# A two-layer graph network on one core: the permutation and the plan of layer two moved into the placing steps, one-hots built from a 16-bit table in SBUF, and two transposes put in front of the relation product

## The reference, cut to what matters

```python
# layer one
msg = h[edge_src] + relvectors[edge_rel]
red = jax.ops.segment_sum(msg, edge_dst, num_segments=h.shape[0])
x = _layernorm(x + _gru_cell(red, h, w_ih, w_hh, b_ih, b_hh))
# layer two
deg_rsqrt = jax.lax.rsqrt(deg)
vals = deg_rsqrt[src] * deg_rsqrt[dst]
msgs = vals[:, None] * (x @ W.T)[dst]
out = jax.ops.segment_sum(msgs, src, num_segments=N)
x = _layernorm(x + out)
```

## Time and profile before

| | |
|---|---|
| time, median of 3 runs (lowest to highest) | 2451.86 us (2450.61 to 2453.98) |
| the profiled execution's own time | 2450.72 us |
| its span, first to last instruction | 2448.7 us |
| busy in the span | PE 2001.0, PE weight loads 1548.1, DVE 1745.1, ACT 831.4, POOL 1628.2 us |
| first and last gather of layer one | 56.1 and 1238.0 us |
| first and last gather of layer two | 1366.2 and 2410.7 us |

### The profile page before, as it was taken

One profiled execution on the slowest core, in us unless ns is written; L12 is line 12 of the kernel. 1 busy time (PEld: TensorE's weight loads), 2 busy tenths in 40 slices (PEclk: granted clock), 3 DMA queues, 4 the chain that ended last, 5 costly groups with the idle time before them and its releaser, 6 DMA issues.

```text
span 2448.7 us, 43994 instructions
## 1 busy us (share of the span) xinstructions
PE 2001.0 (82%) x10013; PEld 1548.1 (63%) x10013; DVE 1745.1 (71%) x2996; ACT 831.4 (34%) x3093; POOL 1628.2 (66%) x1767
## 2 busy tenths in 40 slices
PE   2489898879989769999997589888888888877773
PEld 2366666657666547777774477767676777665552
DVE  5678787788868668888875577767784787544674
ACT  4000000023323226767654366516560665200002
POOL 3677777777777745655510577777777777777774
PEclk7699999989989879999999699999999999999997
DMA  3244444444444335444442433333333333333334
GB/s 97 84 123 149 140 148 143 146 127 149 144 139 145 112 104 148 145 137 141 141 124 79 141 106 107 105 105 106 106 105 105 106 106 105 105 106 106 104 105 149
DMA packets 131522, 296.52 MB, mean 121 GB/s; under 512 B 31024, under 2 KB 64914, under 8 KB 131304
## 3 DMA queue, kind: packets, MB, share of 16 engines
q0 software_dynamic: 80016, 219.06, 31.0%
q10 hardware_dynamic: 35100, 57.62, 7.2%
q1 hardware_dynamic: 16188, 17.21, 2.2%
HBM read 260.91 MB, written 32.85 MB: 120 GB/s over the span
## 4 chain that ended last, share of the span: by engine, by line
PE 34%; POOL 26%; issue 14%; ACT 8%; DMA 8%; DVE 6%; DVEq 1%; SPq 1%; POOLq 0%; ACTq 0%
POOL rows L540 25%; PE ps L1542 19%; ACT rows L1333 6%; DMA rows<-gdram,ids 6%; PE ps L1639 4%; PE ps L1680 3%; DVE rows L700 3%; PE ps L1699 2%; PE ps L1682 2%; PE ps L1671 1%; SPq L398 1%; ACT sums L1482 1%; PE ps L1606 1%; DVEq L761 1%; PE ps L1669 1%
## 5 line engine op out<-in xcount | busy, mean ns | idle before, releaser
L1542 PE MATMUL ps<-rows,onehot 128*128 x5632 | 1372.2, 400 | 206.2 <-SPq L389 124.2
L1542 PEld LDWEIGHTS ps<-rows,onehot 128*128 128x128 f32 x5632 | 1085.8, 197 | 434.3 <-issue 256.2
L540 POOL DMA_INDIRECT rows<-in_x_dram,ids x832 | 796.5, 957 | 344.8 <-issue 245.0
L540 POOL DMA_INDIRECT rows<-gdram,ids x832 | 788.8, 948 | 246.7 <-issue 212.4
L796 DVE TENSOR_TENSOR sums<-sums,ps 128x256 f32 x400 | 168.2, 420 | 332.4 <-PE ps L1542 323.0
L1333 ACT ACTIVATE rows<-rows,a 128x128 f16<-128x128 f16 x624 | 190.8, 388 | 365.7 <-DVE rows L700 365.7
L766 DVE SCALAR_TENSOR_TENSOR onehot<-tkey,node_p,ps 128x512 f32<-128x512 f32 x403 | 298.4, 741 | 13.4 <-issue 10.2
L813 DVE TENSOR_TENSOR sums<-ps,sums 128x800 f16<-128x800 f32 (+1 forms) x156 | 216.3, 1414 | 1.3 <-issue 1.3
L706 DVE SCALAR_TENSOR_TENSOR onehot<-tkey,node_p,ps 128x1024 f32<-128x1024 f32 x154 | 195.7, 1271 | 1.4 <-issue 1.3
L1333 ACT ACTIVATE rows<-rows,b 128x128 f16<-128x128 f16 x624 | 189.5, 386 | 0.0
L1280 ACT COPY sums<-ps 128x256 f32<-128x256 f32 x49 | 18.2, 372 | 502.9 <-PE ps L1598 491.6
(11 more groups left out here) (271 smaller groups left out, 1875.3 us busy)
## 6 DMA issues: line engine op xcount, KB each, us to landing
xpd<-sums ACTq DMA_DIRECT2D x48, 384.0 KB
sums<-xpd ACTq DMA_DIRECT2D x48, 384.0 KB, 3.9
rows<-in_x_dram,ids POOLq DMA_INDIRECT x832, 2.8
rows<-gdram,ids POOLq DMA_INDIRECT x832
xt<-in_x_dram ACTq DMA_DIRECT2D x96, 128.0 KB, 2.2
gdram<-sums ACTq DMA_DIRECT2D x48, 128.0 KB, 1.8
out_dram<-sums SPq DMA_DIRECT2D x6, 896.0 KB
sums<-gdram SPq DMA_DIRECT2D x4, 896.0 KB
```

Of the source, the lines that this page charges most:

```text
L540: pool.indirect_dma_start(rows[:, at:at + D], None, source, bass.IndirectOffsetOnAxis(ap=ids[:, p, s * h + k:s * h + k + 1], axis=0)).then ...
L1542: prod = M.matmul(ps[:, h, 0:width], onehot[:, u % U, k, :], rows[:, bass.ds(at + k * stride, width)], start=(k == 0), stop=(k == q - 1))
```

## The change

Three things are changed. First, the counting is squeezed into 45 steps (52 rounds, so seven steps hold two), the closing of the counts takes two steps, and placing starts at step 55; the plan of layer two and the split of the places are cut into pieces beside placing steps 56 to 62 and later; the first 24 of the 26 batches of chunk 0 lie beside steps 63 to 111, one in two steps, and only two stay in the node steps. Second, the one-hots of counting, placing and permutation are built from `iota_k`, a 16-bit table in SBUF, and from 16-bit keys, and they lie with the key's number innermost; PE, ACT and a reduction on DVE read them and the products with a stride (8 or 16 elements). The 1024- and 512-wide one-hots of the steps themselves (L706, L766) are as before. Third, `sums_over` does its two transposes first and then its two relation products. Besides, POOL's loop for layer two is written chunk by chunk, with the index copy of a chunk's first turn behind the last gathers of the chunk before.

```diff
+COUNTING = 45
+CLOSE = FIRST + COUNTING
+PLACE = CLOSE + 2
+PLAN = PLACE + 1
+PERMUTE = PLACE + 8
+BATCHES = (WIN - PERMUTE) // 2
+SPLIT_LAG = 5
...
+        iota_k = sb("iota_k", [P, G, PB], F16)
...
-        oh_lo = early(2, SUB, P, dt=F16)
-        oh_hi = early(2, SUB, B, dt=F16)
+        oh_lo = early(2, P, SUB, dt=F16)
+        oh_hi = early(2, B, SUB, dt=F16)
...
+            turns = NG1 // S1
+            for g in range(CH):
+                a = g * turns
+                stage(1, S1 * H1, s_tix, a, a % 2)
+                with pool.Fori(0, turns // 2) as i:
+                    for p in range(2):
+                        issue(1, gdram[:, :], S1, H1, D, s_tix, i * 2 + (a + p), (a + p) % 2)
+                issue(1, gdram[:, :], S1, H1, D, s_tix, a + turns - 1, a % 2, False)
...
+                step(V.tensor_copy(hi_16, mask))
+                step(V.scalar_tensor_tensor(a32[:, :], mask, -float(P), lo1, ALU.mult, ALU.add))
+                step(V.tensor_copy(lo_16, a32[:, :]))
+                note(V.tensor_copy(iota_k[:, :, :], iota[:, 0:G].rearrange("p (a k) -> p a k", k=1).to_broadcast([P, G, PB])))
...
             def one_hot(out_ap, keys, count, width):
-                    out_ap, ps[:, 6, 0:width].rearrange("p (a v) -> p a v", a=1).to_broadcast([P, count, width]),
-                    keys.rearrange("p (k a) -> p k a", a=1).to_broadcast([P, count, width]), ALU.is_equal)
+                    out_ap, iota_k[:, 0:width, 0:count],
+                    keys.rearrange("p (v k) -> p v k", v=1).to_broadcast([P, width, count]), ALU.is_equal)
...
             def round_hots(out_ap, keys, r, width):
-                now = keys.rearrange("p (g w) -> p g w", g=CH)[:, :, bass.ds(r * each, each)]
+                now = keys.rearrange("p (g w) -> p g w", g=CH)[:, :, r * each:(r + 1) * each]
                 return V.tensor_tensor(
-                    out_ap.rearrange("p (g i) v -> p g i v", g=CH),
-                    ps[:, 6, 0:width].rearrange("p (g i v) -> p g i v", g=1, i=1).to_broadcast([P, CH, each, width]),
-                    now.rearrange("p g (i v) -> p g i v", v=1).to_broadcast([P, CH, each, width]), ALU.is_equal)
+                    out_ap.rearrange("p v (g i) -> p v g i", g=CH),
+                    iota_k[:, 0:width, 0:each].rearrange("p (v g) i -> p v g i", g=1).to_broadcast([P, width, CH, each]),
+                    now.rearrange("p (v g) i -> p v g i", v=1).to_broadcast([P, width, CH, each]), ALU.is_equal)
...
+                    prod[:, 0, :].rearrange("p (b g i) -> p g i b", g=CH // 2, b=B), axis=AX_X))
...
+            def placing_step(j):
+
+                r = j - PLACE
+                if r < RND:
+                    places(r, r % 2)
+                if r < RND - 1:
+                    buckets_of(r + 1, (r + 1) % 2)
+                if j == PLAN:
+                    plan_columns()
+                if j == PLAN + 1:
+                    degree_roots()
+                if j == PLAN + 2:
+                    plan_nodes()
+                if j == PLAN + 4:
+                    plan_groups()
+                if j == PLAN + 6:
+                    plan_releases()
+                    dve.sem_inc(s_pp, 2)
+                if r >= SPLIT_LAG and (r - SPLIT_LAG) % 4 == 0 and r < SPLIT_LAG + RND:
+                    split_places((r - SPLIT_LAG) // 4)
+                if j == WIN - 2:
+                    chunk_columns()
+                if j >= PERMUTE:
+                    q = (j - PERMUTE) // 2
+                    if (j - PERMUTE) % 2 == 0 and q < BATCHES:
+                        offset_hots(q)
+                    elif (j - PERMUTE) % 2:
+                        bucket_hots(q)
+                x_part(j)
+
+            walk(FIRST, CLOSE, counting_step)
+            walk(CLOSE, PLACE, closing_step)
+            walk(PLACE, WIN, placing_step)
...
+            walk(FIRST, CLOSE, counting_step)
+            walk(CLOSE, PLACE, closing_step)
+            walk(PLACE, WIN, placing_step)
             mark(0)
+            dve.wait_ge(s_pp, BATCHES + 2)
             gates(0, 0)
             tiles = tiles_of(WIN + 2)
             for u in range(U):
-                tiles = node_beside(u, u, tiles, (u, u) if u < 2 else None, u < U - 1)
+                tiles = node_beside(u, u, tiles, BATCHES + u if u < 2 else None, u < U - 1)
             for i in range(4):
                 tiles = tiles_of(i * W8 + (WIN + U + 2))
                 for u in range(W8):
-                    tiles = node_beside(i * W8 + (U + u), u, tiles, batch_at(i, u), u < W8 - 1)
+                    tiles = node_beside(i * W8 + (U + u), u, tiles, None, u < W8 - 1)
             tiles = tiles_of(WIN + U + 4 * W8 + 2)
             for u in range(U):
...
+            for j in range(FIRST, WIN):
+                t, odd = (j - FIRST) // 2, (j - FIRST) % 2
+                if 0 <= j - PLACE < RND:
+                    half_places(j - PLACE)
+                if odd and t + 1 < NT:
+                    copy_x(t + 1)
+                    if t + 3 < NT:
+                        load_x(t + 3, (t + 3) % 2, P if t + 3 < NT - 1 else LAST)
+                if j >= PERMUTE and (j - PERMUTE) // 2 < BATCHES:
+                    scaled((j - PERMUTE) // 2, (j - PERMUTE) % 2)
+                if odd and t < NT:
...
-                    last = M.matmul(ps[:, 4 + a, z:z + B], oh_lo[:, h, q, :], oh_hi[:, h, q, :],
+                    last = M.matmul(ps[:, 4 + a, z:z + B], oh_lo[:, h, :, q], oh_hi[:, h, :, q],
...
+            def placing_step(j):
+
+                r = j - PLACE
+                if r < RND - 1:
+                    place_round(r + 1, (r + 1) % 2)
+                if j == PLAN:
+                    plan_nodes()
+                if j == PLAN + 2:
+                    plan_groups()
+                if j == PLAN + 4:
+                    plan_releases()
+                if j == PLAN + 6:
+                    pe.wait_ge(s_plan_rd, 2)
+                    begin_chunk(0)
+                x_unit(j)
+                if j >= PERMUTE + 2 and (j - PERMUTE) % 2 == 0:
+                    q = (j - PERMUTE) // 2 - 1
+                    pe.wait_ge(s_pm, q * 2 + 2)
+                    batch(q, set_of(q))
...
-                        last = M.matmul(ps[:, 7, w * G:(w + 1) * G], slot[2 + w][:, k, :], slot[1][:, k, :],
+                        last = M.matmul(ps[:, 7, w * G:(w + 1) * G], slot[2 + w][:, k, :], slot[1][:, :, k],
...
                 for c in range(2):
-                    M.matmul(ps[:, 2, c * P:c * P + P], red[:, k, c * P:c * P + P], ident[:, :], start=True, stop=False,
+                    M.matmul(ps[:, 2, c * P:c * P + P], red[:, k, c * P:c * P + P], ident[:, :], start=c == 0, stop=False,
                              is_transpose=True)
-                    last = M.matmul(ps[:, 2, c * P:c * P + P], rel_s[:, c * P:c * P + P], cnT, start=False, stop=True)
+                for c in range(2):
+                    last = M.matmul(ps[:, 2, c * P:c * P + P], rel_s[:, c * P:c * P + P], cnT, start=False, stop=c == 1)
                 last.then_inc(s_rt, 1)
```

409 lines of the change are left out of this document (183 added, 226 removed).

## The result

| | before | changed |
|---|---|---|
| time, median | 2451.24 us (4 runs, 2449.01 to 2453.98) | 2942.3 us (4 runs, 2940.04 to 2944.07) |
| ratio, 95% interval | | 1.2002 (1.1981 to 1.2023) |
| profiled span, mean granted clock | 2448.7 us, 0.933 | 2941.9 us, 0.859 |

The change costs 491 us, where 9 were forecast. Groups by shape of the changed kernel, for the earlier trace rows: line, engine, operation, shapes, count, then busy us, mean ns, idle before.

A forecast was written before the change was run, and what follows sets the result against it. POOL's gathers were taken to bound counting, placing and layer two, PE the node steps. Terms -28 - 39 + 42 + 31 + 1 + 2 = +9 on 2450.7 us gave 2460 us, range 2400 to 2530.

The forecast's parts named there:

- The bound of the kernel before: POOL's gathers bound counting, placing and layer two, as long as its 832 gathers; PE bound the node steps.
- The gap: Between step 111 and node step 1: 54.6 us would shrink to 26.5, so 28 us are gained.
- The node steps: Bound by PE: 24 batches fewer save 33 us, the transposes' new order 6 us, together 39 us less.
- the reorder: In `sums_over`, two transposes before the relation products: 0.15 us off a step, between 0 and 0.25; 39 steps, 6 us.
- The one-hots: On DVE: new ones should take 1.23 (2048), 1.03 (1664), 0.69 (1024) and 0.57 us (800).
- The holds: One-hots with both inputs in SBUF block POOL's gathers: 42 us by step 111, 31 us in layer two.
- the formula: An operation of L us delays POOL's gathers by (L - 0.13)^2 / 2.5 us in the mean.
- the 0.13 us: On DVE and POOL: an operation of L us holds the gathers for L - 0.13 us.
- The strides: PE's batch columns 16 bytes apart: 1.38 to 2.3 us a batch; 0 to 12 us, 2 put in; hidden in layer two.
- PE becomes the bound of placing: Rival: at 2.8 us a batch or more, 2480; from 3.5 us layer two PE-bound too, over 2500; chance 0.09.

The follow-up runs named there:

- e1: Changed kernel with its new schedule, but every one-hot with the width inside and the iota row in PSUM again: 2379.16 us, ratio 0.9706.
- e4: Kernel before, with only both transposes of a tile's sums put in front of the relation product's two passes: 2436.42 us, ratio 0.9941.
- e7: e6 with the iota input of the counting and placing one-hots read from PSUM instead of SBUF: 2412.96 us, ratio 0.9835.
- e14: e1 with the buckets' iota row as 16-bit numbers in SBUF, width inside, run in the disturbed hours: ratio 0.9764.
- e18: Changed kernel with every one-hot's iota input from PSUM, third run, in the disturbed hours: ratio 1.0855 to the kernel before.
- e8: e1 with the bucket one-hots' keys inside in runs of four, both inputs in SBUF: 2439.71 us, ratio 0.9948.
- e6: e1 with the counting and placing one-hots' keys inside and iota from SBUF: 2404.17 us, ratio 0.9802.
- e11: Changed kernel with every one-hot's iota input from PSUM, first run, in the disturbed hours: ratio 1.0831 to the kernel before.
- e9: e1 with the bucket one-hots' keys inside in runs of two, both inputs in SBUF, run in the disturbed hours: ratio 0.9893.
- e2: Changed kernel with the bucket one-hots alone as before, width inside and iota row in PSUM: 2492.31 us, ratio 1.0167.
- e3: Kernel before, with the bucket one-hots alone having the key inside and both inputs in SBUF: 3015.67 us, ratio 1.2298.
- e5: e1 with the offset one-hots' key inside and both inputs in SBUF: 2473.16 us, ratio 1.0097.
- e16: e1 with the key inside for the 2048-wide counting one-hot alone, read as weights, in the disturbed hours: ratio 0.9766.

## Why the prediction was wrong

**The bound of the kernel before.** Right: where nothing is strided (e1), layer two is again as long as its gathers. What failed is that POOL stays the bound after the change.

**The gap.** Right: 26.5 forecast, 25.0 in e1. Timeline of PE in the changed kernel; the first row holds the products of steps 110 and 111, 16 each, so that of step 111 starts near 997:

```profile
991.90 8.95 PE L1586 MATMUL ps<-rows,onehot 128*128 x32
...
1025.67 3.93 PE L1586 MATMUL ps<-rows,onehot 128*128 x16
```

It comes some 147 us late, where 42 were forecast, for PE is now the bound of placing. What follows takes 29 us, near the forecast, with a batch of 5.85 us in it.

**The node steps.** 39 us were forecast, and from node step 1 to the last one e1 saves 41 (325.9 us, where it was 367.0). That is partly luck, for 13 of them are the reorder's, and the 24 batches brought 28, not 33. The changed kernel saves only 29 there (338.1): the two batches left take 5.85 us each. The reorder was mis-sized: 0.15 us a step taken and 0.25 as the bound, 0.34 measured, 15 us instead of 6 (e4). It was read from adjacent transposes alone, which give 0.16; the other 0.18 came from the relation passes, cheaper behind each other than behind a transpose.

**The one-hots.** Right on DVE: 1.23, 1.02, 0.69 and 0.57 us.

**The holds.** Right in kind (e7, e14, e18), and near in size in counting, a turn of 42.9 us (43.5 forecast). That the gathers' mean in layer two came out at 984 ns (985 forecast) is partly luck: the formula takes a gather every 1.25 us, and here one came every 1.74 (1448.2 / 832). Where POOL did run at its own pace, the formula gave 0.32 for 0.5 us a batch (e8). Either the 0.13 us or the assumption that gathers come at any phase fails; no run tells which. That holds lie on the path is right where POOL is the bound (e8, 38 us) and wrong for the changed kernel, where PE is busy 100% of placing and layer two. In counting the rounds' 25 us (e6) would have been paid without holds too (e7, 34). That holds cost nothing in the changed kernel is argued from PE's busy share and from POOL's 285 us of waiting for slots in layer two; the run for it (e11) fell in the disturbed hours, and it stays open.

**The strides, the step that failed.** The prediction took 2 us for them, and as a batch's upper bound 2.3 us, from DVE's strided reduction, 1.6 times an element's time. That row is of an engine that needs about 1 ns an element anyway, and of 32-bit numbers 200 bytes apart. PE takes a column every 0.43 ns when they lie side by side, and 16 bytes apart one every 1.76 (e1, e8, e9): 5.85 us a batch. The rival "PE becomes the bound of placing" named the mechanism and its point of decision, 3.5 us; it had a chance of 0.09, and its times stopped at "over 2500", since no row gave it a size. So the two terms that rested on it fell: 2 us for placing and nothing for layer two, where three steps were to stay under POOL's 7.8 us and take 13.5. Putting the bucket one-hots alone back takes 450 of the 491 us away (e2), changing them alone costs 564 (e3).

**What was not in the sum.** The clock, which falls to a mean of 0.67 behind a strided batch, 2.4 of the 5.7 us that three steps of layer two grew by. ACT's strided reads of the offset one-hots, most of 94 us as soon as PE is not later than ACT (e5). And the strided reads that DVE and ACT do in placing: the reduction takes 884 ns, where it was 570, and a piece of ACT's half 278, where it was 231; what they cost is in the rounds' 25 us (e6).

The parts, put together: e1 2379, rounds +25 (e6) and offsets +94 (e5) make 2498, against 2492 measured with the two together (e2). The buckets' +450 is the difference from there to the changed kernel, so it is no check of its own.

## What to carry to other kernels

When a layout changes for the engine that writes, price it on every engine that reads: here DVE saved some 200 us (1745.1 to 1546.0) off the path, and PE and ACT paid on it. An unknown price bounded by a row of another engine is no bound when that engine is slower by itself; the range must then reach to what the fastest reader would lose. And a part that moved in the same edit can be worth more alone: the schedule and the reorder, with the old layout, are 3% faster than before.

## What the hardware showed that I had not expected

- PE's 16-bit moving columns: 0.43 ns each at 2 bytes, 0.45 at 4, 0.89 at 8, 1.76 at 16; runs of eight side by side with gaps between them cost nothing (336 ns for 400 columns either way).
- Weights 32 bytes apart lengthen a 50-column product from 26 to 60 ns (e16), with the columns 32 bytes apart too it takes 98 (e6).
- Under strided batches the granted clock was 0.84, and behind them 0.67, with PE busy without a break; at 8 bytes (e8) it stayed 1.00.
- ACT reads 128 numbers of 16 bits 0.12 us slower at 16 bytes apart (e5). DVE's reduction of 400 numbers of 32 bits takes 884 ns at 32 bytes apart, 570 side by side.
- DVE operations with both inputs in SBUF hold up POOL's gathers whether they run packed (1.02 us long, gathers' mean 999 ns, e8) or not (1.88 us, 1045 ns, e14); with one input in PSUM the mean stays at 947 to 952.
- Relation passes take 0.41 us each when they alternate with transposes, and 0.32 each behind one another.
